# Two unused SBUF buffers that shift x2, work and h against the expert weights

## The chip, the cores and the metric

The kernel runs on one core of a Trainium2 chip. The metric is the device time of one execution in microseconds (us), the median over several runs. The engines of a core are TensorE (PE; its weight loads are shown apart as PEld), VectorE (DVE), ScalarE (ACT), GpSimd (POOL) and the queues of SyncE (SP).

## The reference, cut to what matters

One layer over 4096 tokens of width 256, in fp32:

```python
x = x + attn(_layernorm(x), w_qkv, w_out)     # causal linear attention: 16 heads of 16, rope, elu + 1
x = x + ffn(_layernorm(x), Wg, Wu, Wd, Wr, temperature)

# ffn: 8 experts of inner width 256, all of them computed, mixed by routing weights
weights = _routing_weights(x, Wr, temperature)
gate = jnp.einsum('btd,edi->beti', x, Wg)
up = jnp.einsum('btd,edi->beti', x, Wu)
h = jax.nn.silu(gate) * up
e_out = jnp.einsum('beti,eid->betd', h, Wd)
out = jnp.einsum('bte,betd->btd', weights, e_out)
```

Three matmuls do most of the arithmetic: gate, up and the product with Wd, for all 8 experts and all tokens.

## The kernel before

**Operands in two parts.** Every fp32 matrix operand is held as a rounded part (`_hi`) and a remainder (`_lo`), both of type float32r with 4 bytes for an element. A product is the sum of three matmuls: hi by hi, lo by hi and hi by lo. ACT writes a hi part, POOL or DVE the lo part.

**Tiling.** Tokens go in blocks of 512 (`B`) for the experts and in tiles of 128 (`P`) for the attention. A unit is one expert and one half of its inner width: 16 units (`UNITS`) for each of 8 blocks, 128 in all. For a unit, `gate(n)` and `up(n)` call `three` (L436): six matmuls each, in which a 128x128 tile of the gate or up weights is the stationary operand and `x2` (the normed tokens, transposed) moves, 512 columns at a time (L440). DVE and ACT make `h` of the two (`silu` L668, `h_up` L1060, `h_hi` L676, POOL `h_lo` L1216), all by way of the buffer `work` (its first half is `hb`). `down(n)` (L465) then has 12 matmuls: here a 128x128 tile of `h` is stationary, and 256 columns of `wd` move (L474). `acc` (L1066) adds the weighted result to `xa`.

**Order.** Each engine has its own program, written out by hand. After a prologue, 31 steps `s` interleave the attention of one token tile with four units (L489 to L494). On TensorE a step reads: gate, up, qkv (L300 and L301), gate, state (L371), av (L352, L340), down, up, down, o_T (L383), gate, proj (L396), up, gate, down, scores (L323), x2_T (L408), down, up. The last units (L496 to L498) run without attention, and the last two of them take `x2` instead of `h_hi` and `h_lo` as the place of h (`h_at`, L232) and the banks R0 to R3 as output. `up(n)` waits at L459 to L461 for DVE: for `h_up` of the unit ahead and, where its bank also held the transposed tokens, for `x2_lo` (L945), the last of DVE's three operations after scores and x2_T: `mask`, `mask`, `x2_lo` (L1109).

**Where the buffers lie.** `sb` (L73) takes the buffers one after the other in a partition of SBUF, in the order of the program (L80 to L145), each rounded up to 32 bytes. The start addresses in bytes, as the built programs have them:

| buffer | role at TensorE | before | mod 512 | after | mod 512 |
|---|---|---|---|---|---|
| wqkv_hi, wqkv_lo | moving, L300/L301 | 18560, 24704 | 128 | same | 128 |
| wout_hi, wout_lo | moving, L396 | 30848, 32896 | 128 | same | 128 |
| wr_s | stationary, L421 | 34944 | 128 | same | 128 |
| wg, wu (hi and lo) | stationary, L440 | 35072 to 84224 | 256 | same | 256 |
| wd_hi, wd_lo | moving, L474 | 100608, 116992 | 256 | same | 256 |
| xo_hi, xo_lo | stationary, L300/L301 | 135424, 137472 | 256 | same | 256 |
| ox_hi, ox_lo | stationary, L396 | 177088, 178112 | 448 | same | 448 |
| xa | - | 181056 | 320 | same | 320 |
| x2_hi, x2_lo | moving, L440 and L421 | 193344, 201536 | 320 | 193664, 201856 | 128 |
| router | - | 209728 | 320 | 210048 | 128 |
| work | - | 212256 | 288 | 212800 | 320 |
| h_hi, h_lo | stationary, L474 | 220448, 224544 | 288 | 220992, 225088 | 320 |

All tiles of 128x128 and all moving slices of these buffers begin at a whole multiple of 512 bytes from the buffer's start. So each pair of operands has one distance modulo 512, called its **offset** here: start of the stationary tile less start of the moving slice.

Of the kernel before, what the change touches and what calls it, by code (L numbers as in the profile page):

```python
# [15 lines left out]
P = 128  # L16
# [53 lines left out]
def build(nc, x, xT, w_qkv, w_out, Wg, Wu, Wd, Wr, temperature, tab, out):  # L70
    ctx = ExitStack()

    def sb(name, shape, dt=F32):  # L73
        return ctx.enter_context(nc.sbuf_tensor(name, shape, dt))
# [4 lines left out]
    with ctx:  # L79
# [51 lines left out]
        st_x = sb("st_x", [P, NP, 3, W1], BF16)  # L131

        xa = sb("xa", [P, NXA, D])
        x2 = [sb(f"x2_{s}", [P, 2, KD, B], F32R) for s in ("hi", "lo")]
        rt = sb("router", [P, 2 * E, NT, E])
        R = {n: rt[:, i, :, :] for i, n in enumerate(
# [3 lines left out]
        lg_rows = rt[:, :, :, :].rearrange("p i t e -> p (i t e)")  # L140
        wo = sb("wo", [P, 2, NT, E])

        work = sb("work", [P, 4, B])
        hb, stage = work[:, 0:2, :], work[:, 2:4, :]
        h_p = [sb(f"h_{s}", [P, 2, B], F32R) for s in ("hi", "lo")]  # L145
# [1205 lines left out]
```

## Time and profile before

| | |
|---|---|
| median of 3 runs | 804.74 us (804.35 to 805.25) |
| time of the profiled execution | 803.15 us |
| its span, first to last instruction | 801.3 us |
| mean granted TensorE clock | 0.972 of full |
| PE busy | 757.1 us, 94% of the span |
| DVE, ACT, POOL busy | 607.4, 466.4, 482.8 us |
| DMA | 38.27 MB, mean 48 GB/s |

The profile lists busy times by engine, groups of instructions by line, the chain of work that ended last, and instructions in order of time. A matmul's shown duration includes its way through the array and overlaps with its neighbours, so two that follow each other are compared by the distance of their starts, called a **step** here. The start column of the timeline gives it to 0.01 us, so it is read over a row of equal matmuls.

### The profile page before, as it was taken

The page shows a single profiled execution, that of the slowest core. Times are in us where ns is not written, and L with a number is a line of the kernel's source. Part 1 is how long each engine was busy: PE and PEld are TensorE (multiplying, and loading weights), DVE is VectorE, ACT ScalarE, POOL GpSimd, SP SyncE. Part 2 cuts the span into 40 slices and gives each one's busy share as a digit, 9 for nine tenths or more (in the row PEclk, how much of TensorE's full clock was granted, in tenths as well). Part 3 has the DMA queues.
Part 4 walks back from the last instruction along what each step waited for, and adds up shares of the span by engine and source line. Part 5 has one row for each costly group of instructions (what it writes and reads, how often), then busy time and mean ns, then how long its engine had stood idle before and what let it go on. Part 6 is the DMA issues. An engine that isn't in the chain of part 4 may idle for free.

```text
span 801.3 us, 18061 instructions
## 1 busy us (share of the span) xinstructions
PE 757.1 (94%) x6660; PEld 651.1 (81%) x6660; DVE 607.4 (76%) x1597; ACT 466.4 (58%) x886; POOL 482.8 (60%) x537
## 2 busy tenths in 40 slices
PE   4375899999999999999999999999999999999998
PEld 3264688888888888888888888888888888888887
DVE  6788888878877797779877797777877788756243
ACT  3664766666566656666665565666656665634222
POOL 3686678765666665655666665565676656653322
PEclk8776999999999999999999999999999999999999
DMA  4544134122110122122101221120211121100000
GB/s 140 128 99 110 49 77 94 39 44 68 41 34 17 35 66 41 41 43 51 37 22 41 43 68 41 41 43 12 58 41 41 41 54 29 27 1 27 1 1 27
DMA packets 97319, 38.27 MB, mean 48 GB/s; under 512 B 74192, under 2 KB 96976, under 8 KB 97232
## 3 DMA queue, kind: packets, MB, share of 16 engines
q1 hardware_dynamic: 90704, 30.83, 17.4%
q10 hardware_dynamic: 6528, 6.29, 2.7%
q8 instruction: 53, 0.87, 0.4%
q14 instruction: 34, 0.28, 0.1%
HBM read 16.13 MB, written 4.19 MB: 25 GB/s over the span
## 4 chain that ended last, share of the span: by engine, by line
PE 87%; DVE 5%; POOL 2%; ACT 2%; issue 2%; DMA 1%; DVEq 0%; ACTq 0%; SPq 0%; POOLq 0%
PE y L474 22%; PE gate L440 21%; PE up L440 21%; PE front L300 5%; PE back L352 3%; PE front L301 3%; PE back L396 3%; PE up L371 2%; POOL a_lo L1187 1%; PE up L408 1%; PE front L323 1%; PE front L421 1%; PE back L340 1%; PE back L383 1%; PE back L323 1%
## 5 line engine op out<-in xcount | busy, mean ns | idle before, releaser
L1216 POOL TENSOR_TENSOR h_lo<-work,h_hi 128x512 fp32r<-128x512 f32 x126 | 163.2, 1295 | 60.2 <-ACT h_hi L676 60.2
L1187 POOL TENSOR_TENSOR a_lo<-am,a_hi 128x512 f16<-128x512 f32 x120 | 144.5, 1206 | 53.7 <-ACT a_hi L603 51.0
L474 PE MATMUL y<-wd_hi,h_hi 128*128 128x256 f32 x504 | 146.4, 290 | 0.0
L474 PE MATMUL y<-wd_lo,h_hi 128*128 128x256 f32 x504 | 142.1, 282 | 0.0
L474 PE MATMUL y<-wd_hi,h_lo 128*128 128x256 f32 x504 | 141.2, 280 | 0.0
L1060 DVE TENSOR_TENSOR work<-work,up 128x512 f32<-128x512 f32 x128 | 87.0, 679 | 71.1 <-PE up L440 70.7
L1076 DVE SCALAR_TENSOR_TENSOR xa<-y,wo,xa 128x256 f32<-128x256 f32 x252 | 111.9, 470 | 2.0 <-PE y L474 2.0
L676 ACT ACTIVATE h_hi<-work 128x512 fp32r<-128x512 f32 x126 | 79.4, 630 | 57.8 <-DVE work L1060 35.6
L474 PEld LDWEIGHTS y<-wd_hi,h_hi 128*128 128x128 f32 x504 | 94.9, 188 | 4.1
L474 PEld LDWEIGHTS y<-wd_lo,h_hi 128*128 128x128 f32 x504 | 94.8, 188 | 2.9
L603 ACT ACTIVATE a_hi<-am 128x512 f16<-128x512 f32 x120 | 74.9, 625 | 35.4 <-DVE am L838 35.3
L474 PEld LDWEIGHTS y<-wd_hi,h_lo 128*128 128x128 f32 x504 | 95.1, 189 | 0.0
L668 ACT ACTIVATE work<-gate 128x512 f32<-128x512 f32 x128 | 75.7, 592 | 30.3 <-PE gate L440 18.6
L1175 POOL TENSOR_TENSOR vs<-vs,vx 128x256 f32<-128x256 f32 x32 | 21.7, 680 | 105.5 <-ACT vx L590 105.5
L440 PE MATMUL gate<-x_hi,wg_hi 128*128 128x512 f32 x256 | 82.6, 404 | 0.3 <-ACT work L668 0.3
L440 PE MATMUL up<-x_hi,wu_hi 128*128 128x512 f32 x256 | 81.8, 401 | 0.0
L440 PE MATMUL gate<-x_hi,wg_lo 128*128 128x512 f32 x256 | 79.9, 394 | 0.0
L440 PE MATMUL gate<-x_lo,wg_hi 128*128 128x512 f32 x256 | 79.9, 393 | 0.0
L440 PE MATMUL up<-x_hi,wu_lo 128*128 128x512 f32 x256 | 79.8, 393 | 0.0
L440 PE MATMUL up<-x_lo,wu_hi 128*128 128x512 f32 x256 | 79.5, 392 | 0.0
L1166 POOL TENSOR_TENSOR rop<-qk,tabs 128x256 f32<-128x256 f32 x64 | 45.2, 726 | 34.1 <-ACT qk L548 34.1
L440 PEld LDWEIGHTS gate<-x_hi,wg_lo 128*128 128x128 f32 x256 | 48.4, 189 | 10.9
(220 smaller groups left out, 1734.9 us busy)
## 6 DMA issues: line engine op xcount, KB each, us to landing
xr<-xT SPq DMA_DIRECT2D x32, 128.0 KB, 2.5
xa<-x SPq DMA_DIRECT2D x32, 128.0 KB, 2.7
out<-xa SPq DMA_DIRECT2D x32, 128.0 KB, 1.7
xa<-Wg ACTq DMA_DIRECT2D x8, 256.0 KB, 2.8
work<-Wd ACTq DMA_DIRECT2D x8, 256.0 KB, 2.9
work<-Wu ACTq DMA_DIRECT2D x8, 256.0 KB, 2.8
work<-w_qkv SPq DMA_DIRECT2D x2, 384.0 KB, 3.9
qT<-q_st SPq DMA_TRANSPOSE x32, 3.2
```

The source lines that it names most:

```text
L300: pe.matmul(qk_bank(g)[:, :], lhs, wqkv_p[wi][:, k, 0:2 * D], start=first, stop=last)
L301: m = pe.matmul(R1[:, 0:D], lhs, wqkv_p[wi][:, k, 2 * D:], start=first, stop=last)
L440: m = pe.matmul(ps, weights[wi][:, e_, k, m_ * P:(m_ + 1) * P], x2[xi][:, b % 2, k, :], start=(n == 0), stop=(n == 3 * KD - 1))
L474: m = pe.matmul(y_bank(n, t), h_at(hi, n)[:, t * P:(t + 1) * P], wd_p[wi][:, u // KI, u % KI, :], start=(n % KI == 0 and (t % 2 == 0 or n ...
L603: act.activation(a_p[0][:, heads(r), :], am_place(g, r).rearrange("p (h n) -> p h n", h=4), ACT.Copy).then_inc(s_ahi, 1)
L668: act.activation(hb[:, n % 2, :], G[:, :], ACT.Silu).then_inc(s_g, 1)
L676: act.activation(h_at(0, n), hb[:, n % 2, :], ACT.Copy).then_inc(s_hhi, 1)
L1060: v.tensor_tensor(hb[:, n % 2, :], hb[:, n % 2, :], U[:, :], ALU.mult).then_inc(s_h, 1)
L1076: v.scalar_tensor_tensor(out=xs, in0=y_bank(n, t), scalar=wo[:, b % 2, t, e_:e_ + 1], in1=xs, op0=ALU.mult, op1=ALU.add).then_inc(s_acc, 1)
L1166: pool.tensor_tensor(r2_h[:, :, half, :], qk_h[:, :, 1 - half, :], bcast(tabs[:, g // NT % 2, g % NT, at:at + HALF], 1, 2 * H), ALU.mult). ...
L1187: pool.tensor_tensor(a_p[1][:, heads(r), :], am_place(g, r).rearrange("p (h n) -> p h n", h=4), a_p[0][:, heads(r), :], ALU.subtract).then ...
L1216: pool.tensor_tensor(h_at(1, n), hb[:, n % 2, :], h_at(0, n).bitcast(F32), ALU.subtract).then_inc(s_hlo, 1)
```

## The change

Two buffers that no instruction reads or writes are allocated, of 320 and 224 bytes in a partition. All that is allocated behind them moves: `x2` by 320 bytes, and `work` and `h` by 544. No instruction is added, removed or moved on any engine, and no wait; only addresses in the instructions differ.

```diff
         xa = sb("xa", [P, NXA, D])
+        sb("x2_gap", [P, 80])
         x2 = [sb(f"x2_{s}", [P, 2, KD, B], F32R) for s in ("hi", "lo")]
...
         wo = sb("wo", [P, 2, NT, E])
 
+        sb("h_gap", [P, 56])
         work = sb("work", [P, 4, B])
```

The offset of gate and up (L440) goes from 256 - 320 = -64 to 256 - 128 = +128, that of down (L474) from 288 - 256 = +32 to 320 - 256 = +64, that of the logit rows (L421) from -192 to 0, and that of the last two units' down from 320 - 256 = +64 to 128 - 256 = -128. qkv (+128) and proj (448 - 128, which is -192) keep theirs. `x2`, `work` and `h` keep or gain a start at a multiple of 64 bytes; before, `work` and `h` lay 32 bytes off one.

## Rows read from the trace of the kernel before

**Rows 1.** The page: busy us (share of the span) and instructions of each engine.
```profile
PE 757.1 (94%) x6660; PEld 651.1 (81%) x6660; DVE 607.4 (76%) x1597; ACT 466.4 (58%) x886; POOL 482.8 (60%) x537
```

**Rows 2.** Windows: us; busy of PE, PEld, DVE, ACT, POOL; PE clock; DMA share; GB/s.
```profile
0.00:82.00 82.00, 44.97 (x474) 33.91 (x475) 63.52 (x162) 44.85 (x94) 52.53 (x72) 0.75 0.48 118
...
176.00:268.00 92.00, 92.00 (x834) 79.89 (x832) 73.25 (x196) 56.97 (x109) 57.61 (x65) 1.00 0.19 42
...
726.00:801.00 75.00, 71.55 (x419) 62.46 (x417) 33.47 (x86) 23.14 (x39) 20.81 (x17) 1.00 0.04 15
```

**Rows 3.** The page's groups of down and of gate and up, with counts.
```profile
L474 PE MATMUL y<-wd_hi,h_hi 128*128 128x256 f32 x504 | 146.4, 290 | 0.0
...
L440 PE MATMUL gate<-x_hi,wg_hi 128*128 128x512 f32 x256 | 82.6, 404 | 0.3 <-ACT work L668 0.3
```

**Rows 4.** Timeline of PE at the end: start us, us; down with h, then with x2.
```profile
793.25 0.28 PE L474 MATMUL y<-wd_hi,h_hi 128*128 128x256 f32 x1
...
794.67 0.28 PE L474 MATMUL front<-wd_hi,x_hi 128*128 128x256 f32 x1
...
797.27 0.28 PE L474 MATMUL back<-wd_hi,x_lo 128*128 128x256 f32 x1
```

**Rows 5.** Timeline of PE in a full step: the first and last matmul of a down.
```profile
401.95 0.28 PE L474 MATMUL y<-wd_hi,h_hi 128*128 128x256 f32 x1
...
403.25 0.28 PE L474 MATMUL y<-wd_hi,h_lo 128*128 128x256 f32 x1
```

**Rows 6.** Timeline of PE: logit rows (16 stationary columns), then a gate and down's first.
```profile
726.30 0.62 PE L421 MATMUL front<-x_hi,wr_s 128*16 128x512 f32 x2
...
727.22 0.62 PE L440 MATMUL gate<-x_hi,wg_hi 128*128 128x512 f32 x2
...
730.42 0.62 PE L440 MATMUL gate<-x_hi,wg_hi 128*128 128x512 f32 x2
...
731.80 0.28 PE L474 MATMUL y<-wd_hi,h_hi 128*128 128x256 f32 x1
```

**Rows 7.** Timeline of PE: first matmul of a qkv and what follows, two blocks.
```profile
340.17 0.40 PE L300 MATMUL front<-wqkv_hi,xo_hi 128*128 128x512 f32 x1
...
342.28 0.40 PE L440 MATMUL gate<-x_hi,wg_hi 128*128 128x512 f32 x1
...
409.90 0.39 PE L300 MATMUL front<-wqkv_hi,xo_hi 128*128 128x512 f32 x1
...
411.98 0.39 PE L440 MATMUL gate<-x_hi,wg_hi 128*128 128x512 f32 x1
```

**Rows 8.** Timeline of a step's end: scores, DVE's operations, the up that waits.
```profile
403.98 1.29 DVE L838 TENSOR_TENSOR am<-front,cmask 128x512 f32<-128x512 f32 x2 [1.20 <-PE front L323]
...
405.18 0.41 DVE L945 TENSOR_TENSOR x_lo<-up,x_hi 128x256 fp32r<-128x256 f32 x1
...
405.48 0.19 PEld L474 LDWEIGHTS y<-wd_hi,h_lo 128*128 128x128 f32 x1
405.60 0.28 PE L474 MATMUL y<-wd_hi,h_lo 128*128 128x256 f32 x1
405.65 0.30 PEld L440 LDWEIGHTS up<-x_hi,wu_hi 128*128 128x128 f32 x2
405.71 0.67 PE L440 MATMUL up<-x_hi,wu_hi 128*128 128x512 f32 x2
...
406.22 0.63 PE L440 MATMUL up<-x_hi,wu_lo 128*128 128x512 f32 x2
```

**Rows 9.** Groups by line and form: POOL's subtractions over work, h and xa.
```profile
L1216 POOL TENSOR_TENSOR h_lo<-work,h_hi 128x512 fp32r<-128x512 f32 x126 | 163.2, 1295 | 60.2 <-ACT h_hi L676 60.2
...
L1132 POOL TENSOR_TENSOR wg_lo<-xa,wg_hi 128x512 fp32r<-128x512 f32 x8 | 10.4, 1295 | 2.5 <-ACT wg_hi L532 2.5
```

**Rows 10.** Timeline of PE: part of a proj, and the up behind it.
```profile
421.37 0.40 PE L396 MATMUL back<-wout_lo,ox_hi 128*128 128x256 f32 x2
...
421.85 0.62 PE L440 MATMUL up<-x_hi,wu_hi 128*128 128x512 f32 x2
```

## The prediction, made before the changed kernel was run

> **What bounds the kernel now.** I read the page first, then the windows by stage, and then single steps in the timeline, since a change of addresses can only act through how long an instruction takes. The page has PE at 94% of an 801.3 us span [rows 1]. The windows tell where [rows 2]: in the first 82 us PE is busy for 45 us and others set the time. In a full stretch (176 to 268 us) it is busy 92.00 of 92.00 us, with DVE at 73, ACT at 57 and POOL at 58. In the last 75 us it is busy 71.55. So from about 82 us to the end nearly every nanosecond on TensorE counts, and nothing else does unless it makes PE wait. There the clock stands at 1.00 of full, the 2.4 GHz level. Two lines carry the matmuls that the change touches: down (L474) with three groups of 504, 1512 in all, and gate and up (L440) with six groups of 256, 1536 in all [rows 3].
>
> The number to look for is the step, the distance of two starts. Twelve matmuls of 256 columns in down, with h at its own place, start from 793.25 to 794.67: 1.42 / 12 = 118.3 ns each [rows 4]. In a full step of the kernel eleven steps take 403.25 - 401.95 = 1.30, or 118.2 [rows 5]. So it is the same whether the other engines are busy or nearly idle. Gate takes 731.80 - 730.42 = 1.38 us for six of 512 columns, 230 ns [rows 6]. At 2.4 GHz 256 and 512 columns are 106.7 and 213.3 ns, so there are 11.6 and 16.7 ns in each step that columns alone don't explain.
>
> **Down, offset +32 to +64.** The trace of before holds the new offset already. The last two units keep h in x2, whose stationary tiles lie at 320 modulo 512 while wd lies at 256: +64, and both residues are what the change gives h and wd. Their 24 matmuls start from 794.67 to 797.27, 23 steps in 2.60 us: 113.0 ns [rows 4]. The twelve ahead of them, same weights, same shape, same idle neighbours, take 118.3. What else differs is the output bank (R0 to R3 in place of Y0 and Y1). I take the offset as the cause: within either kind several matmuls in a row write one bank, and proj writes one of the very banks used at the end (R3) and doesn't reach 113: four steps in 421.85 - 421.37 = 0.48 us, 120 ns, at offset -192 [rows 10]. The saving is 118.3 - 113.0 = 5.3 ns, for the 11 steps inside a unit 58 ns, and for the 126 units with h at its own place 126 x 0.058 = **-7.3 us**.
>
> Where does it go? In each of the 27 full steps one of the four downs stands between scores and the last up. That up waits for DVE: two masks start at 403.98 when scores are done, x2_lo follows from 405.18 for 0.41 us, to 405.59, and the weight load of up starts at 405.65, while the matmul ahead of it started at 405.60 [rows 8]. The load at 405.48 starts 0.12 ahead of its own matmul, as loads in this stream do; this one starts 0.06 ahead of its own, at 405.71, so it is already some 0.05 us late, and the two matmuls behind it take 406.22 - 405.71 = 0.51 us in place of 0.46. DVE's three operations hang on scores, not on down. A down that is 58 ns shorter there only makes up wait 58 ns longer: 27 x 0.058 = **+1.6 us** given back. The other three downs of a step have nothing late behind them in the timeline, and the chain behind each hangs on PE itself.
>
> **Gate and up, offset -64 to +128.** Here too the trace has the new offset: in qkv xo lies at 256 and wqkv at 128, the very residues that wg, wu and x2 get. A qkv block is six of 512 columns and six of 256. Two blocks take 2.11 and 2.08 us [rows 7], and the 27 from 87 us on are of these two lengths (or 0.01 more), 2.10 on average. At the steps of today's gate and down it would be 6 x (230 + 118.3) = 2.09 us. So +128 costs 0.013 / 6 = 2.2 ns for a pair of 512 and 256. If all of it belongs to the 512 columns, gate and up lose 2.2 ns in a step, if none, nothing; I take half, 1.1 ns. Some 1,300 of the 1536 are followed by a load at this offset (the others by a load of h, k_st or a transpose): 1300 x 1.1 = **+1.4 us**, with bounds at 0 and +2.9. A gain isn't excluded by this but has no row: no qkv block runs faster than 2.08 us, and a gate at the 224 ns that two of 113 would make would leave 6 x 6 = 36 ns in a block to see.
>
> **The rest.** The last 24 matmuls go to offset -128, of which no row tells. Between 113 and 120 ns a step that is 0 to +0.2 us; I take +0.1. The logit rows are 32 matmuls, a ns or two each: nothing. They have one use, though: four of them take 727.22 - 726.30 = 0.92 us, 230 ns, with a load of only 16 columns for most of them [rows 6]. So not all of the excess comes from the length of the load, and a cure by offset need not carry over from 256 to 512 columns. On the other engines work and h become aligned to 64 bytes. POOL's subtraction takes 1295 ns over work and h (off by 32) and 1295 over xa and wg (aligned) [rows 9], so I put that at nothing; it would be hidden under PE in any case.
>
> **The sum.** -7.3 + 1.6 + 1.4 + 0.1 = -4.2 us. The profiled execution took 803.15 us (span 801.3 and 1.9 around it), so its like would be 799.0. The median of the runs is 1.6 above it, and I forecast 804.74 - 4.2 = **800.5 us**.
>
> **Rivals.** (a) No change. The 113 ns belong to the end of the program (other banks, or h in x2 in some other way), and offsets do nothing, as the equal rates of qkv, gate and proj to a ns or two would allow. Time 804.7. Against it: nothing else in the trace runs at 113 in a row, and the switch comes from one matmul to the next with the change of buffer. The Trainium skill, "TensorE: Matmul & The Clock Gate", section on the steps of a matmul, says this outright: the moving operand and the weight load have independent read ports, and loading the next tile takes no bandwidth from the running matmul. By that rule no offset could matter. The 118 beside 113 ns speak against it, and no run here has yet separated bank and offset. I give it 0.17.
> (b) Slower. Down gains as said, net 5.7 us with the part given back, but gate and up lose more. This decides at 5.7 / 1300 = 4.4 ns in a step, 234.4 ns. If a gate at +128 went to 236 ns, +6 ns, it would be 7.8 - 5.7 + 0.1 = +2.2, or 806.9. For it: x2 streams twice the columns of a down, and qkv's mix of forms hides how it is shared. Against it: that would need 36 ns more in a qkv block than [rows 7] show. The other way to a slower kernel is that down gains nothing and gate loses its 1.1 to 2.2 ns: 804.7 + 1.4 to 2.9 = 806.1 to 807.6. Together 0.12.
> (c) More than forecast. The wait at the last up isn't as hard as I read it and gate loses nothing: 804.74 - 7.3 = 797.4. If +128 gave a gate the whole saving in spite of qkv, 1300 x 6 = 7.8 us more would go, about 793. 0.13 together, the second a small part.
> (d) The forecast, in its bounds of 798.9 to 802.0 (gate's loss 0 to 2.9 us): 0.58.
>
> **How the numbers follow.** A measurement of this kernel tells 0.2%, 1.6 us, from no change. Faster than 803.1: all of (c) and (d), 0.71. Slower than 806.4: most of (b), 0.11. Between: 0.18. For 8 in 10 the range goes from 797.0, under the first form of (c), to 805.5, over (a).
>
> **What would show it.** In the profile of after, a down's twelve matmuls should take 1.36 to 1.37 us in place of 1.42, at equal clock, in full steps and at the end alike; were they still at 1.42, (a) is right. Six of gate should take 1.38 to 1.39; 1.41 is (b), 1.35 is the far end of (c). The last up of a step should have its weight load start some 0.1 us behind the matmul before it in place of 0.05, and x2_lo should end just ahead of that load. The first 82 us should be as long as before. The last 24 matmuls should have lost their 113 ns, now that x2 lies elsewhere. I would be wrong most simply if the period of the effect is not 512 bytes, so that h at its new place is not like x2 at its old one.

## The result, and the profile after

The changed kernel takes 805.91 us (20 runs, 804.35 to 806.64), against 804.46 for the kernel before beside it (20 runs). The ratio is 1.0017, with a 95% interval of 1.0011 to 1.0024: 1.4 us slower, where 4.2 us faster was forecast. Its profiled execution has a span of 804.7 us.

Two windows of after, with the same columns as [rows 2]:

```profile
176.00:268.00 92.00, 92.00 (x831) 79.33 (x831) 72.83 (x197) 56.56 (x109) 57.47 (x64) 1.00 0.19 42
...
726.00:805.00 79.00, 75.15 (x445) 65.66 (x443) 34.08 (x88) 24.85 (x43) 22.44 (x18) 1.00 0.04 14
```

PE is again busy for the whole of a full stretch, at the full clock, yet with 831 instructions in the 92 us in place of 834. So the time was lost on PE or in its waits, though "busy" shows no wait in either kernel.

The end of the program in after, which answers to [rows 4] (start and duration in us; L474 is now L476):

```profile
796.72 0.28 PE L476 MATMUL y<-wd_hi,h_hi 128*128 128x256 f32 x1
...
798.14 0.27 PE L476 MATMUL front<-wd_hi,x_hi 128*128 128x256 f32 x1
...
800.87 0.28 PE L476 MATMUL back<-wd_hi,x_lo 128*128 128x256 f32 x1
```

The last 24 matmuls, now with x2 at its new place, take 2.73 / 23 = 118.7 ns a step in place of 113.0, with the same output banks. So the address did it, not the bank. But the twelve with h ahead of them, which got the offset of +64, take 1.42 / 12 = 118.3, no less than before. In a full step a down looks like this:

```profile
305.44 0.28 PE L476 MATMUL y<-wd_hi,h_hi 128*128 128x256 f32 x1
...
306.04 0.28 PE L476 MATMUL y<-wd_hi,h_lo 128*128 128x256 f32 x1
...
306.72 0.28 PE L476 MATMUL y<-wd_hi,h_lo 128*128 128x256 f32 x1
```

The first five steps take 0.60 us, 120 ns each; the six behind them take 0.68 us, 113 ns each. At this offset a down has two rates and changes over within a unit. In 81 of its 126 units more than half of the steps take 115 ns or less, in the other 45 nearly none; in the kernel before no unit gets there. A whole gate (first matmul, then down's first behind it, as in [rows 6]) takes 1.40 us in place of 1.38:

```profile
733.96 0.63 PE L442 MATMUL gate<-x_hi,wg_hi 128*128 128x512 f32 x2
...
735.36 0.28 PE L476 MATMUL y<-wd_hi,h_hi 128*128 128x256 f32 x1
```

The mean over the starts of all matmuls says the same. It is taken from 95 us to the end, without the steps that are longer because of a wait or because matmuls of another type run ahead of them. Those are over 150 ns in down (55 of some 1390 in either kernel) and over 250 ns in gate and up (29 and 34 of 630 each); most of them are the first step of a block.

| step, ns | before | after | count |
|---|---|---|---|
| down to down | 118.4 | 116.1 | 1330 |
| gate to gate | 230.0 | 231.9 | 601 |
| up to up | 230.1 | 232.2 | 596 |
| qkv to qkv, 512 columns (not moved) | 231.2 | 231.3 | 156 |

Over the 26 steps from one qkv at 87 us to the last at 686 us, the sums of steps by kind in the two traces are:

| us | before | after | difference |
|---|---|---|---|
| whole stretch | 598.8 | 601.6 | +2.8 |
| inside down | 137.7 | 135.1 | -2.6 |
| inside gate | 121.8 | 122.7 | +1.0 |
| inside up | 121.5 | 123.8 | +2.3 |
| inside proj | 15.6 | 16.6 | +0.9 |
| last of down to scores | 5.5 | 6.5 | +1.0 |

The last line is one wait for a transposed tile (1.0 us, once), which this execution has and the other hasn't. The stretch ahead of the first qkv differs by 0.8 us more (87.98 against 87.15 us). Without these two the profiled spans lie 1.6 us apart in place of 3.4, as the medians do with 1.4.

Inside proj and up are waits. The last up of a full step, which answers to [rows 8], in the timeline of all engines:

```profile
407.90 0.42 DVE L947 TENSOR_TENSOR x_lo<-up,x_hi 128x256 fp32r<-128x256 f32 x1
...
408.27 0.28 PE L476 MATMUL y<-wd_hi,h_lo 128*128 128x256 f32 x1
408.37 0.30 PEld L442 LDWEIGHTS up<-x_hi,wu_hi 128*128 128x128 f32 x2
408.38 0.72 PE L442 MATMUL up<-x_hi,wu_hi 128*128 128x512 f32 x2
...
408.95 0.39 PE L442 MATMUL up<-x_hi,wu_lo 128*128 128x512 f32 x1
```

x2_lo ends at 408.32, the load starts at 408.37, 0.10 us behind the matmul at 408.27, and the two first matmuls of up take 0.57 us in place of 0.51. The lag of a load is the time from the start of the matmul ahead of it to its own start. The median lag of this one over the 20 steps from 176 to 636 us is 94 ns, against 53 before. That part was foreseen. This one wasn't, although the profile of before has it (k_lo, which writes k_st, and o_lo on DVE, then proj's first weight load with the wait it ended in brackets, and PE's matmuls; first before, then after):

```profile
419.97 0.68 DVE L848 TENSOR_TENSOR k_st<-front,k_st 128x512 f16<-128x512 f32 x1
...
420.56 0.41 DVE L900 TENSOR_TENSOR ox_lo<-back,ox_hi 128x256 fp32r<-128x256 f32 x1
...
421.03 0.30 PEld L396 LDWEIGHTS back<-wout_hi,ox_hi 128*128 128x128 f32 x2 [0.18 <-DVE ox_lo L900]
421.13 0.41 PE L396 MATMUL back<-wout_hi,ox_hi 128*128 128x256 f32 x2
...
421.37 0.28 PE L396 MATMUL back<-wout_lo,ox_hi 128*128 128x256 f32 x1
```
```profile
423.82 0.30 PEld L398 LDWEIGHTS back<-wout_hi,ox_hi 128*128 128x128 f32 x2 [0.19 <-DVE ox_lo L902]
423.90 0.43 PE L398 MATMUL back<-wout_hi,ox_hi 128*128 128x256 f32 x2
...
424.17 0.39 PE L398 MATMUL back<-wout_lo,ox_hi 128*128 128x256 f32 x2
```

In after the first two matmuls of proj take 424.17 - 423.90 = 0.27 us, against 421.37 - 421.13 = 0.24 before. The lists of waits of before and of after (engine and line waited for: us in total, times, longest) give it a row of its own for PEld; for PE they have a single wait of 0.7 us for it:

```profile
PEld back L396 <- DVE ox_lo L900: 5.8, 27, 1.1
```
```profile
PEld back L398 <- DVE ox_lo L902: 6.8, 27, 1.1
```

### The profile page after: what moved, and what is told of

Read it like the earlier page. It is cut to its first block, busy times and chain, and to the rows that moved or that the text cites. A ratio compares the mean times of both kernels' runs of the same rounds, so it can differ in the third digit from the quotient of the medians.

```text
span 804.7 us, 18061 instructions
## 1 busy us (share of the span) xinstructions
PE 759.6 (94%) x6660; PEld 649.8 (81%) x6660; DVE 605.3 (75%) x1597; ACT 465.8 (58%) x886; POOL 482.1 (60%) x537
## 4 chain that ended last, share of the span: by engine, by line
PE 87%; DVE 6%; ACT 2%; issue 2%; POOL 2%; DMA 1%; SPq 0%; DVEq 0%; ACTq 0%; POOLq 0%
PE up L442 21%; PE y L476 21%; PE gate L442 21%; PE front L302 5%; PE front L303 3%; PE back L354 3%; PE back L398 3%; PE up L373 2%; PE up L410 1%; PE front L325 1%; PE front L423 1%; PE back L342 1%; PE back L385 1%; POOL a_lo L1189 1%; PE back L325 1%
## 5 line engine op out<-in xcount | busy, mean ns | idle before, releaser
L1218 POOL TENSOR_TENSOR h_lo<-work,h_hi 128x512 fp32r<-128x512 f32 x126 | 163.1, 1294 | 60.1 <-ACT h_hi L678 60.1
L476 PE MATMUL y<-wd_hi,h_hi 128*128 128x256 f32 x504 | 146.0, 290 | 0.0
L476 PE MATMUL y<-wd_lo,h_hi 128*128 128x256 f32 x504 | 140.7, 279 | 0.0
L476 PE MATMUL y<-wd_hi,h_lo 128*128 128x256 f32 x504 | 140.5, 279 | 0.0
L476 PEld LDWEIGHTS y<-wd_hi,h_hi 128*128 128x128 f32 x504 | 95.0, 188 | 4.3
L476 PEld LDWEIGHTS y<-wd_lo,h_hi 128*128 128x128 f32 x504 | 94.8, 188 | 2.9
L476 PEld LDWEIGHTS y<-wd_hi,h_lo 128*128 128x128 f32 x504 | 95.4, 189 | 0.0
```

The lines of the kernel that those rows point to most:

```text
L476: m = pe.matmul(y_bank(n, t), h_at(hi, n)[:, t * P:(t + 1) * P], wd_p[wi][:, u // KI, u % KI, :], start=(n % KI == 0 and (t % 2 == 0 or n ...
L1218: pool.tensor_tensor(h_at(1, n), hb[:, n % 2, :], h_at(0, n).bitcast(F32), ALU.subtract).then_inc(s_hlo, 1)
```

## The experiments

Two theories stood against each other. **The rate is all**: the time follows the sum of the steps' changes. **Waits take it back**: what down saves between qkv and proj, and between scores and the last up, is lost at two loads that wait for DVE, while what gate and up lose elsewhere is lost for good. A third question is what function of the offset the step is. The runs of the next two parts are timed beside the kernel before; ratios have 95% intervals, and us are the ratio times 804.5.

### One part of the change alone

h alone (label h_only):

```diff
+        sb("h_gap", [P, 8])
         work = sb("work", [P, 4, B])
```

> Only work and h move, by 32 bytes: down's offset goes from +32 to +64 as in the changed kernel, gate and up stay at -64. In the changed kernel a down's steps average 116.1 ns against 118.4 before. Theory 'the rate is all': 1386 steps inside units x 2.3 ns = -3.2 us, so 801.3. Theory 'waits take it back': in each of 27 full steps two of the four downs lie between qkv and proj, where proj waits for DVE's o_lo, and one between scores and the last up, which waits for x2_lo; only the fourth counts (27 x 25 ns = 0.7 us), and the units before and behind the full steps add 0.4: -1.1 us, so 803.4, with the last up's load 0.09 us behind the matmul ahead of it as in the changed kernel (0.05 before).

Measured: 0.9975 (0.9966 to 0.9985), -2.0 us. Down's steps average 115.8, gate 230.0, up 229.9 ns. In the stretch of 26 steps down gave 2.7 us, and all but 0.2 of it is gone: inside up +1.1, inside proj +1.0, the rest in small parts. The lag of the last up's load went from 53 to 92 ns, that of proj's first load from 125 to 195. Behind that stretch, from the last qkv to the last matmul, it took 110.3 us in place of 111.3, where the wait theory had put 0.4 us for the units on both sides of it. Ahead of it these profiles differ by more than a microsecond without regard to the change, so nothing is read there. So the rate is not all. The measured gain lies between the two theories and nearer to the waits, which have the mechanism and had the end of the program too small.

x2 alone (label x_only):

```diff
+        sb("x2_gap", [P, 80])
         x2 = [sb(f"x2_{s}", [P, 2, KD, B], F32R) for s in ("hi", "lo")]
...
+        sb("h_gap", [P, 48])
         work = sb("work", [P, 4, B])
```

> Only x2 moves, by 320 bytes (a second gap puts work and h back to 288 modulo 512): gate and up go from -64 to +128, down stays at +32, the last two units' down goes from +64 to -128. Both theories: gate and up at 232.0 in place of 230.0 ns, some 1300 steps, +2.6 us, and +0.1 for the last two units: 807.2. If gate's loss in the changed kernel came instead from down's new rate or from waits, gate stays at 230 and the time at 804.5 to 804.9.

Measured: 1.0028 (1.0017 to 1.0039), +2.3 us. Gate 232.5, up 231.9, down 118.5, and 118.5 in the last two units in place of 113.4. The lag of proj's load shrank to 90 ns, and of its 27 waits in the list 2 are left (1.6 us): PE now comes later there than DVE. The loss of gate and up is their own. The two parts together make +0.3 us, the change measured +1.4; each interval is some 0.8 us to either side, so this is no contradiction and no proof that the parts add. The traces come closer: over the 26 steps, without the one wait of 1.0 us that x2 alone has in its trace too, the parts make -0.2 and +1.7 us, and the change +1.8.

### The wait at the last up taken away

In the kernel before (label before_swap), DVE's order at L1109:

```diff
-                h_up(n + 2); route_both(router); ln2(c); mask(a, 0); mask(a, 1); x2_lo(c); route_out(router)
+                h_up(n + 2); route_both(router); ln2(c); mask(a, 0); x2_lo(c); mask(a, 1); route_out(router)
```

> The kernel before, with DVE doing x2_lo(c) ahead of mask(a, 1) in place of behind it. x2_lo is then ready some 0.25 us earlier and the last up of a step no longer waits. Theory 'waits': the 0.05 us by which its load is late goes, 27 x 0.05 = -1.3 us, 803.2, unless the later mask(a, 1) makes a new wait. Theory 'the rate is all': the late load costs nothing, 804.5.

Measured: 0.9977 (0.9967 to 0.9988), -1.9 us. The end of a step in the timeline:

```profile
405.83 0.42 DVE L945 TENSOR_TENSOR x_lo<-up,x_hi 128x256 fp32r<-128x256 f32 x1 [0.24 <-ACT x_hi L633]
...
406.52 0.28 PE L474 MATMUL y<-wd_hi,h_lo 128*128 128x256 f32 x1
406.52 0.31 PEld L440 LDWEIGHTS up<-x_hi,wu_hi 128*128 128x128 f32 x2
406.64 0.62 PE L440 MATMUL up<-x_hi,wu_hi 128*128 128x512 f32 x2
...
407.09 0.39 PE L440 MATMUL up<-x_hi,wu_lo 128*128 128x512 f32 x1
```

x2_lo runs ahead of the second mask and is done at 406.25; the load starts with the matmul ahead of it (406.52), and the first two of up take 0.45 us in place of 0.51. Inside up the 26 steps lost 1.6 us.

The same swap in the changed kernel (label after_swap):

> The changed kernel with the same swap on DVE. Theory 'waits': the last up's load is 0.09 us late there, so 27 x 0.09 = -2.5 us from 805.9, to 803.4, and half as much again as the swap brings to the kernel before. Theory 'the rate is all': no more than for the kernel before.

Measured: 0.9992 (0.9982 to 1.0002) of the kernel before, -0.6 us, which is 2.0 less than the changed kernel. Inside up 2.6 us went, a whole us more than in the kernel before, as the longer lag asked; in the times the two gains (2.0 and 1.9) can't be told apart. The traces tell them apart: the load's lag is 53 and 94 ns without the swap, and gone in both with it.

### Other offsets

Each kernel of this set has two gaps that differ only in size. The six whose labels begin with s were run once, for their steps; the two called x0_h64 are the same kernel without and with the swap on DVE, and were timed. The expectations first, then one table for all.

> Gaps that put gate and up at offset 0 and down at +128. Read for the steps alone. Theory 'one function of the offset modulo 512', from what is seen: +128 is a poor offset for down as for qkv (119 to 120 ns), and gate at 0 is between 230 and 233 as the logit rows at 0 (232.9). Rival 'alignment': only the 32-byte start of h was bad, and down is at 116 at any multiple of 64.

> Gate and up at +64, down at +192. One function of the offset: +64 was the good one for down, so gate should go below 230, to 225 to 228; the logit rows at +64 in the changed kernel (233.1, 14 steps) speak against it. Down at +192: unknown, 116 to 120. Alignment: gate 230 to 232, down 116.

> Gate and up and down at 256. No row has this offset. One function: both kinds move the same way from their best; alignment: gate 230 to 232, down 116.

> Gate and up at +192, down at 0. The last step of a gate before down's load at +192 took 232 in the changed kernel, and the last step of a down before up's load at 0 took 115 to 116. One function: gate 231 to 233, down 115 to 116. Alignment: gate 230 to 232, down 116.

> Gate and up at -192, down at -64, read for the steps. The last step of a gate before proj's load at -192 took 226.8 in the changed kernel, proj itself runs at 116 to 118 there: gate 227 to 230. Down at -64: 117.7 in the last units of one run: 117 to 118.

> Gate and up at -128, down at -192, read for the steps. Gate before a load at -128 took 235 in one place (26 steps): gate 231 to 235. Down at -192 as proj, 116 to 118.

> Gate and up at offset 0 (228.7 ns in the look at it, 230.0 before), down at +64 again, but with work and h 544 bytes on from their place in the kernel before, not 32. If the period is 512 bytes, down's steps are 116 as with 32; if not, something else. Time, rates times what counts: gate and up -1.3 ns on some 1300 steps, of which the three blocks between qkv and proj are given back at proj's wait once down is short as well (5 of 8 count): -1.1; down -1.8 as measured with h alone: 801.5. Theory 'the rate is all': -1.7 - 3.2 = -4.9, 799.4.

> The same with x2_lo ahead of mask(a, 1) on DVE. Theory 'waits': the last up's load, 0.09 us late without the swap, is no longer late: 27 x 0.09 = -2.4 us, 799.1. Theory 'the rate is all': as without the swap.

Sizes of the two gaps in 4-byte elements, and mean steps in ns as in the table of the result; "last" is the down of the last two units, 23 steps, whose offset is the negative of gate's. Where an expectation has the logit rows at two offsets: the second tile of `wr_s` lies 64 bytes behind the first, so half of these matmuls are 64 bytes on from the offset given at the top.

| label | x2_gap, h_gap | gate, up at | gate | up | down at | down | last |
|---|---|---|---|---|---|---|---|
| before | 0, 0 | -64 | 230.0 | 230.1 | +32 | 118.4 | 113.4 |
| after | 80, 56 | +128 | 231.9 | 232.2 | +64 | 116.1 | 118.5 |
| s1_0_128 | 112, 40 | 0 | 228.9 | 228.5 | +128 | 119.9 | 119.3 |
| s2_64_192 | 96, 72 | +64 | 233.7 | 233.0 | +192 | 117.9 | 117.7 |
| s3_256_256 | 48, 8 | 256 | 229.5 | 229.8 | 256 | 119.4 | 120.0 |
| s4_192_0 | 64, 56 | +192 | 229.9 | 231.3 | 0 | 119.5 | 117.8 |
| s5_m192_m64 | 32, 72 | -192 | 233.6 | 233.0 | -64 | 117.8 | 117.8 |
| s6_m128_m192 | 16, 56 | -128 | 232.0 | 232.0 | -192 | 116.1 | 118.5 |
| x0_h64 | 112, 24 | 0 | 229.4 | 229.6 | +64 | 117.4 | 120.0 |
| x0_h64_swap | 112, 24 | 0 | 229.2 | 230.0 | +64 | 117.3 | 120.0 |

The single times of the six were 802.6, 806.9, 804.5, 806.6, 806.9 and 804.9 us, from s1 to s6, beside 804.2 for the kernel before (803.6, of 15 runs, for the last two).

**The period is 256 bytes.** s6 and the changed kernel differ by 256 in both offsets, and agree in every column to 0.1 ns or so (gate 231.95 and 231.92, up 232.03 and 232.17, down 116.13 and 116.12), and the 26 steps take 600.3 and 601.6 us, of which 1.0 is the one wait that s6 hasn't. s5 and s2 do too: 233.6 and 233.7, 233.0 and 233.0, 117.8 and 117.9. s3 and s4 have down at the same place and agree in it (119.4 and 119.5), though their gates lie at different offsets. It is less exact where the other product's offset differs: up at -64 and at +192 takes 230.1 and 231.3. Alignment is not the cause either: all offsets but the +32 have these buffers at a multiple of 64 bytes, and down's mean spreads over 4 ns there. The texts of the expectations that used a period of 512 missed: s5's gate at -192 was expected at 227 to 230 and is as slow as at +64, which is the same place. The first theory also missed s1's gate (230 to 233 expected, 228.9 measured), s2's (below 230, 233.7) and s4's (231 to 233, 229.9), and s4's down (115 to 116, 119.5); s5's down and both numbers of s6 came as expected.

**The good offset of down is not that of gate.** Modulo 256 gate and up are best at 0 (228.5 to 230), then 192 (230 to 231), then 128 (232), worst at 64 (233 to 234). Down is best at 64, then 192, then 32, and worst at 0 and 128. The function is not one and the same for both kinds, as s1 to s4 had it in their expectations. The changed kernel gave down its best place and gate and up their second worst.

**Down at +64 is not one rate.** It averages 115.8 in h_only, 116.1 in the changed kernel and in s6, and 117.4 in x0_h64. The share of units that reach 113 differs: 90, 81, 80 and 16 of 126 have more than half of their steps there. x0_h64 differs from h_only in the offset of gate and up, and in h only by 512 bytes. So gate's better offset cost some of down's. The last two units show the same. In the kernel before they run at 113 throughout; in s4, where they lie at -192, which is +64 modulo 256, all 23 steps are at 117 to 119 ns.

x0_h64 took 0.9980 (0.9972 to 0.9989) of the kernel before, -1.6 us, and x0_h64_swap 0.9966 (0.9952 to 0.9979), **-2.7 us**: 800.96 beside 803.64. Both are faster than the kernel before. Both gained less than either theory had it: 3.0 and 5.1 us were expected without the swap, 5.4 and 5.1 with it. One reason is that down did not keep its 116. With it went part of the swap's worth: the lag without the swap is 61 ns and not 92, and the swap took 1.1 us out of up, about what it brought in the times.

## Why the prediction was wrong

Each step of the sum, in us, and what was measured for it:

| term | predicted | measured |
|---|---|---|
| down, rate of +64 | -7.3 (5.3 ns) | -3.1 (2.3 ns x 1386 steps inside units) |
| given back at the last up | +1.6 | +1.1 (27 x (94 - 53) ns) |
| given back at proj | 0 | +0.9 |
| gate and up, rate of +128 | +1.4 (1.1 ns) | +2.6 (2.0 ns x 1300) |
| last two units | +0.1 | +0.1 (23 x 5.1 ns) |
| sum | -4.2 | +1.6, with 1.4 in the medians |

**Down's rate** failed first, and by the most: 5.3 ns a step in the sum, 2.3 measured. The prediction said "The trace of before holds the new offset already" and took 113.0 ns from the last 24 matmuls. The residues were right, and the address was the cause, as it had argued. But these 24 follow each other without a break, and the same place has two rates, 113 and 118, of which such a stream stays in one: in s4 it stays in the other. So they are a single sample, and were read as 24. The trace of before had the second sample: proj [rows 10] lies at -192, which is +64 modulo 256, and averages 118.0 (the four steps shown there, at 120, are one block of 28). The prediction set proj aside by taking 512 as the period, which it named as its weakest point, and did not test against that row.

**"The other three downs of a step have nothing late behind them"** failed second. Two of them stand between qkv and proj, and proj's first load ends a chain through ACT and DVE that starts at qkv, not at the downs: q_lo, k_lo, o_lo. The traces show it: o_lo starts 8.70 us behind the last matmul of qkv in the kernel before (median of 23 steps), 8.71 with h alone and 8.70 in the changed kernel, while the o_hi that it also needs is done 0.17, 0.21 and 0.21 us ahead of it. The load ran 125 ns behind the matmul ahead of it, and that was just hidden. In these three traces the first step of proj is 116 to 121 ns as long as the lag is at most 124 ns, and grows with it above that: 126 ns at a lag of 139, 145 at 146, 180 at 180. 50 ns less on PE ahead of the load made the lag 174 and came out as a longer first step of proj. The row was in the list of waits of before all along, under PEld; PE's own list has one wait of 0.7 us of it, and PE counts as busy all through. No run took this wait away, as the swap did with the other; what shows it is the constant 8.70 us and the lags.

**Gate's rate** had the right row, sign and bounds (0 to 2.2 ns), and the choice inside them was too low: 2.0 measured. The half was right for the qkv block itself, where the steps of 512 columns take 231.2 ns (1.2 over gate's 230.0) and those of 256 some 119.1. But gate and up at the same offset take 231.9 and 232.2: the price in a block that mixes two forms did not carry over to blocks of one form. Why, no run shows.

**The sign.** Together these turned a gain into a small loss. Had gate's 2.0 and down's 2.3 been known but not the second wait, the sum would have been 0.7: no change. Rival (b) came nearest, with the right mechanism (gate loses more than down nets) at other prices. Rival (a), that offsets do nothing, falls: 118.5 in the last units with the same banks, and x2 alone makes the kernel slower by 0.28%. The rule beside it, of the Trainium skill, "TensorE: Matmul & The Clock Gate", section "Step-by-step: what each phase is for", is that loading the next tile takes no read bandwidth from the running matmul. It has no room for an effect of addresses, and this case has one: same instructions, same clock, other addresses, and the step goes from 228.5 to 233.7 ns. The addresses move the step by 2% for 512 columns and by 6% for 256. Whether it is the load that takes the time, no run shows.

Three small slips in the prediction's working change nothing in the forecast. Two steps of 113 ns make 226, not 224. The low end of the sum is 799.1 with its own terms (-7.3 + 1.6 + 0.1), not 798.9. The far end of rival (c), about 793, is 800.5 - 7.8 and leaves in the 1.4 us that gate would then not lose; without them it is 791.3.

**What held:** the last up's load went from 0.05 to 0.09 us late as foreseen, POOL's subtraction didn't change (h_lo 1294 ns, against 1295 in [rows 9]), and x2_lo is indeed the last wait there, as the swap shows.

**What stays open:** what makes a down fall into the 113 ns stream or leave it, and which part of the memory has the period of 256 bytes. No run here changed what runs ahead of a down and nothing else. Nor was a weight buffer moved: all runs moved x2 and h against weights that stayed. That the distance counts, and not the moved buffer's own address modulo 256, is supported only by proj, whose buffers lie at other residues (448 and 128) at the same distance of 64 and which runs at 115 to 118 ns as down does there. The steps from one kind to the next speak against a simple rule of distance. The last step of a gate, with down's load behind it, has a median of 235, 227 and 226 ns where x2 stays in place and h lies at 32, 64 and 0 modulo 256 (before, h_only, s4; 36 steps each). So the place of the next tile counts there too. But at a distance of 64 it is 226 ns in x0_h64, where a step inside gate takes 233.7, and at 192 it is 226 in s4 and 232 in the changed kernel. The table by offset holds for the steps inside a block.

## What to carry to other kernels

A run of equal instructions without a break is one sample, however many there are: before its rate is carried to another place, find a second stretch with the same relation, and check the period that makes two places "the same". On an engine that is busy without a gap, look for weight loads that wait (PEld in the list of waits, and a load that starts well behind the matmul ahead of it): they mark where another engine already keeps pace, and time saved on TensorE ahead of such a point is not saved. A shift of buffers is cheap to try and worth 0.3% either way at most here; removing one wait of 50 ns in each step was worth as much.

## What the runs showed of the hardware

With float32r operands the mean step of a 128x128x512 matmul at the full granted clock went from 228.5 (s1) to 233.7 ns (s2), and that of a 128x128x256 one from 113.4 (before) to 120.0 (s3, x0_h64; the last two units in each), by nothing but the addresses of its operands. Within a block the mean repeats when the buffers move by 256 bytes (s5 and s2, s6 and the changed kernel). Whether it is the distance of the two operands or the address of the moved one that counts is open, as said above. At a distance of 64 bytes the shorter one has two rates, 113 and 118 ns, and keeps either over 6 to 24 matmuls.
